# Merged mask and maximum products in a second attention, and one-hot tiles moved from VectorE to GpSimd

## What is computed

```python
a = _mha(inputs, inputs, inputs, Wk1, Wv1, Wq1, Wo1, bo1, masked=True)    # 256 x 256, causal, 16 heads
a = _layernorm(inputs + a, g1, b1)
c = _mha(context_seq, context_seq, a, Wk2, Wv2, Wq2, Wo2, bo2, masked=False)
c = _layernorm(c + c, g2, b2)
...
probs = softmax(x @ w_router)                  # 8 experts, top 1 of them used, the 8th adds nothing
out = 2 * top_value * expert(x)[top_index]     # 7 routed experts, hidden 512
return out + (x @ ws_up * silu(x @ ws_gate)) @ ws_down
```

## Time and profile before

| what | us |
|---|---|
| median of 3 runs | 335.74 (334.33 to 340.63) |
| the profiled execution | 338.23 |
| its span, first to last instruction | 336.1 |
| TensorE busy | 291.7 (87%) |
| VectorE busy | 257.9 (77%) |
| ScalarE busy | 209.6 (62%) |
| GpSimd busy | 152.2 (45%) |
| mean granted TensorE clock | 0.946 of full speed |

### The profile page before, as it was taken

The page is one execution under the profiler, slowest core; times in us unless marked ns, Lnnn a source line. Parts: engine busy times, 40 slices in busy tenths (PEclk is TensorE's granted clock), DMA queues, the critical chain, the costliest instruction groups (busy, mean ns, idle before and its releaser), DMA issues.

```text
span 336.1 us, 8921 instructions
## 1 busy us (share of the span) xinstructions
PE 291.7 (87%) x3475; PEld 222.8 (66%) x3475; DVE 257.9 (77%) x694; ACT 209.6 (62%) x442; POOL 152.2 (45%) x157
## 2 busy tenths in 40 slices
PE   5787957599999998989998999775898999999994
PEld 5655746455656645777776787544655999759993
DVE  4699977874664897977999577789689996894832
ACT  3665973445469649777867999234763648745561
POOL 9902898546344111443434345312431666432551
PEclk9999976958999999997999999799699999999998
DMA  7600223522400000000000000000002202040211
GB/s 249 252 2 1 97 96 100 180 98 91 137 0 2 0 0 4 2 2 2 2 2 3 2 2 3 2 0 0 3 3 108 82 4 97 2 168 21 90 41 32
DMA packets 6609, 16.64 MB, mean 50 GB/s; under 512 B 676, under 2 KB 2984, under 8 KB 6568
## 3 DMA queue, kind: packets, MB, share of 16 engines
q1 hardware_dynamic: 6568, 16.08, 13.6%
HBM read 10.83 MB, written 0.52 MB: 34 GB/s over the span
## 4 chain that ended last, share of the span: by engine, by line
PE 52%; DVE 31%; ACT 5%; POOL 4%; issue 4%; DMA 1%; SPq 0%; DVEq 0%; ACTq 0%
PE ps L808 8%; PE ps L810 7%; PE ps L809 7%; DVE MX L1400 6%; PE ps L1037 5%; DVE prl L667 3%; DVE stat L1355 2%; POOL prl L667 2%; PE ps L869 2%; PE ps L1129 2%; PE ps L870 2%; PE ps L881 2%; PE ps L1025 2%; PE ps L1099 2%; DVE pr L1576 2%
## 5 line engine op out<-in xcount | busy, mean ns | idle before, releaser
L667 POOL TENSOR_TENSOR prl<-pr,prh 128x384 f16<-128x384 f32 (+1 forms) x48 | 49.4, 1029 | 76.0 <-ACT pr L1188 76.0
L1185 ACT ACTIVATE prh<-ps 128x384 f16<-128x384 f32 (+1 forms) x96 | 51.2, 534 | 17.6 <-PE ps L810 6.6
L1400 DVE TENSOR_REDUCE MX<-ps 128x8 f32<-128x512 f32 (+2 forms) x80 | 52.1, 682 | 8.3 <-PE ps L911 4.5
L672 POOL TENSOR_TENSOR prl<-pr,prh 128x512 f16<-128x512 f32 x28 | 32.7, 1171 | 43.6 <-ACT prh L1225 43.6
L777 POOL TENSOR_TENSOR wl<-wraw,wh 128x512 f16<-128x512 f32 (+1 forms) x30 | 33.5, 1137 | 18.1 <-DVE wh L1288 18.0
L667 DVE TENSOR_TENSOR prl<-ps,prh 128x384 f16<-128x384 f32 (+1 forms) x48 | 28.5, 594 | 6.3 <-ACT ps L1188 5.9
L1576 DVE TENSOR_TENSOR pr<-ps,hr 128x512 f32<-128x512 f32 x28 | 19.0, 685 | 11.9 <-ACT hr L1219 10.7
L819 PE MATMUL ps<-cst 128*128 128x128 f32 x120 | 21.9, 321 | 4.7 <-DMA cst<-in_const 4.1
L1188 ACT ACTIVATE ps<-ps 128x384 f32<-128x384 f32 (+1 forms) x48 | 25.8, 538 | 0.0
L1188 ACT ACTIVATE pr<-ps 128x384 f32<-128x384 f32 (+1 forms) x48 | 25.6, 533 | 0.0
L1219 ACT ACTIVATE hr<-ps 128x512 f32<-128x512 f32 x28 | 16.5, 597 | 13.6 <-PE ps L810 12.8
(11 more groups left out here) (256 smaller groups left out, 1045.2 us busy)
## 6 DMA issues: line engine op xcount, KB each, us to landing
wraw<-in_weights SPq DMA_DIRECT2D x8, 768.0 KB, 4.0
wraw<-wh SPq DMA_DIRECT2D x6, 384.0 KB, 2.6
wraw<-wl SPq DMA_DIRECT2D x6, 384.0 KB, 3.0
wraw<-in_weights SPq DMA_DIRECT2D x2, 576.0 KB, 7.3
rowb<-in_rows SPq DMA_DIRECT2D x1, 708.0 KB, 4.6
wd<-in_down SPq DMA_DIRECT2D x1, 576.0 KB, 7.3
X<-in_x SPq DMA_DIRECT2D x2, 256.0 KB, 4.0
picks<-in_spread SPq DMA_DIRECT2D x1, 512.0 KB, 5.0
```

The source lines that it names most:

```text
L667: return engine.tensor_tensor(prl[:, g, three, 0:width], whole, prh[:, g, three, 0:width], ALU.subtract)
L672: return engine.tensor_tensor(hlo[:, g, k % NPV, :], hh[:, g, k % 2, :], hhi[:, g, k % NPV, :], ALU.subtract)
L1185: nc.scalar.activation(high, src[:, 0:width], ACT.Exp, scale=SCALE[a]).then_inc(pr_ready, 1)
L1400: nc.vector.tensor_reduce(o, src[:].rearrange("p (h k) -> p h k", h=heads), AX_X, ALU.max).then_inc(max_read, 1)
```

## The change

1. In the second attention the two mask products (columns 0 and 256) become one matmul of 2 x 128 columns, and the two that add the negated maxima become one of 384 columns. For that MT holds 384 columns, with the last 128 queries twice; `negmax` makes the third block with one more matmul, and its copy on ScalarE is 384 wide where a = 1. The columns in all stay the same.
2. `onehot_t` is issued by GpSimd, as the same tensor_scalar with the same waits. In the cost table it stands as 1.0 on GpSimd instead of 0.42 on VectorE.

```diff
--- before.py
+++ after.py
@@ -256,7 +256,7 @@
             "split_low": [("pool", 1.25)], "plow_pool": [("pool", .95 if e[1:2] == (1,) else 1.22)], 
             "lo1": [("pool", 1.17)], "xsplit": [("act", .6), ("pool", 1.2)], "rank": [("pe", .5), ("dve", 2.6)],
             "onehot": [("dve", 2.2)], "spill": [("dve", 1.2)], "sort_high": [("pe", .87), ("act", .6)], "sort_low": [("pe", .87), ("dve", .7)],
-            "spots": [("pe", .25), ("act", .6)], "onehot_t": [("dve", .42)],
+            "spots": [("pe", .25), ("act", .6)], "onehot_t": [("pool", 1.0)],
             "downr": [("pe", .72), ("act", .29), ("dve", .3)], "back": [("pe", .52)],
             "turn": [("pe", .95), ("act", 1.2 if e[1:2] in (("x1",), ("x3",)) else .6), ("dve", .69)], "v1": [("pe", .8), ("act", .65), ("dve", .69)], "bias_split": [("dve", 1.6)], "square": [("pe", 1.), ("dve", .69 if e[1:2] != ("v1",) else 1.45)],
             "negmax": [("dve", .6), ("pe", .3), ("act", .4)], "pv": [("pe", .3)], "out_norm": [("dve", .78)],
@@ -531,7 +531,7 @@
         VS = [sb("VSh", [P, G, T, H, DV], F16), sb("VSl", [P, G, T, H, DV], F16)]
         MX = sb("MX", [P, B, 2, H])
         MP = sb("MP", [P, B, 2, P], BF16)
-        MT = sb("MT", [P, B, S], BF16)
+        MT = sb("MT", [P, B, S + P], BF16)
         pr = sb("pr", [P, G, 2, GT])
         prh = sb("prh", [P, G, NPV, GT], F16)
         prl = sb("prl", [P, G, NPV, GT], F16)
@@ -783,6 +783,13 @@
                     g = e[1]
                     pool.wait_ge(x_high, n)
                     nc.gpsimd.tensor_tensor(xhl[g][:, 1], lnx[:, g], xhl[g][:, 0], ALU.subtract).then_inc(x_ready, 1)
+                elif kind == "onehot_t":
+                    _, g, s = e
+                    pool.wait_ge(spots_ready, nth[("spots", g)])
+                    for kind_, done in (("sort_high", sorted_high_mm), ("sort_low", sorted_low_mm)):
+                        pool.wait_ge(done, 3 * (g + 1))
+                    nc.gpsimd.tensor_scalar(onehot_t[:, s, :], spotsT[g], consts("part", 10)[:, s:s + 1], None,
+                                            ALU.is_equal).then_inc(onehot_t_ready, 1)
                 elif kind == "plow_pool":
                     pool.wait_ge(prh_ready, nth[("scores",) + e[1:]])
                     make_low(nc.gpsimd, e).then_inc(prl_ready[kind], 1)
@@ -932,8 +939,8 @@
                     pe.wait_ge(masks1_ready, 1)
                     pe.wait_ge(neg_ready, n)
                     take(bank[e][0], negT_ready, n)
-                    for t in range(2):
-                        mm = nc.tensor.matmul(o[:, t * P:(t + 1) * P], MP[:, e[2], t, :], identb[:], start=True, stop=True)
+                    for i, t in enumerate((0, 1, 1) if e[1] == 1 else (0, 1)):
+                        mm = nc.tensor.matmul(o[:, i * P:(i + 1) * P], MP[:, e[2], t, :], identb[:], start=True, stop=True)
                     mm.then_inc(neg_mm, 1)
                 elif kind == "scores":
                     _, a, b, u = e
@@ -952,7 +959,7 @@
                                              KBX[:, p // 2, b, 2 * (p % 2):2 * (p % 2) + 2, :].rearrange("p h k -> p (h k)"),
                                              QS[:, g, p // 2, q0:q0 + S], start=True, stop=False)
                             mm = nc.tensor.matmul(o[:, i * S:(i + 1) * S],
-                                                  pairsel[:, 2 * p:2 * p + 2, :].rearrange("p h k -> p (h k)"), mt,
+                                                  pairsel[:, 2 * p:2 * p + 2, :].rearrange("p h k -> p (h k)"), mt[:, 0:S],
                                                   start=False, stop=True)
                     else:
                         kb = kbs[:, b % 2]
@@ -960,10 +967,9 @@
                         kw = dict(start=False, stop=True, skip_group_check=True)
                         nc.tensor.matmul(o[:, 0:S], kb[:, j, h, 0:P], QS[:, g, j, q0:q0 + S], start=True, stop=True)
                         nc.tensor.matmul(o[:, S:S + P], kb[:, j, h, P:2 * P], QS[:, g, j, q0 + P:q0 + S], **kw)
-                        nc.tensor.matmul(o[:, 0:S], headsel[:, u:u + 1].broadcast_to([P, P]), mt, **kw)
-                        nc.tensor.matmul(o[:, S:S + P], headsel[:, u:u + 1].broadcast_to([P, P]), mt[:, P:S], **kw)
-                        for c in (0, S):
-                            mm = nc.tensor.matmul(o[:, c:c + P], identb[:], trib[:, 1, :], **kw)
+                        nc.tensor.matmul(o[:, 0:S + P], headsel[:, u:u + 1].broadcast_to([P, P]), mt, **kw)
+                        mm = nc.tensor.matmul(o[:].rearrange("p (c k) -> p c k", k=S)[:, :, 0:P], identb[:],
+                                              trib[:, 1, :].unsqueeze(1).broadcast_to([P, 2, P]), **kw)
                     mm.then_inc(sc_mm, 1)
                 elif kind == "pv":
                     _, a, b, u = e
@@ -1172,7 +1178,8 @@
                     nc.scalar.copy(VS[0][:, g, :, :, 0:D], src[:].rearrange("p (t h d) -> p t h d", t=T, d=D)).then_inc(v1_high, 1)
                 elif kind == "negmax":
                     sc.wait_ge(neg_mm, n)
-                    nc.scalar.copy(MT[:, e[2], :], src[:, 0:S]).then_inc(negT_ready, 1)
+                    width = S + P if e[1] == 1 else S
+                    nc.scalar.copy(MT[:, e[2], 0:width], src[:, 0:width]).then_inc(negT_ready, 1)
                 elif kind == "scores":
                     _, a, b, u = e
                     g = b // 2
@@ -1527,13 +1534,6 @@
                     for t in range(T):
                         ins = nc.vector.tensor_scalar(onehot[:, t, :], slots, pos[:, t:t + 1], None, ALU.is_equal)
                     ins.then_inc(onehot_ready, 1)
-                elif kind == "onehot_t":
-                    _, g, s = e
-                    dve.wait_ge(spots_ready, nth[("spots", g)])
-                    for kind_, done in (("sort_high", sorted_high_mm), ("sort_low", sorted_low_mm)):
-                        dve.wait_ge(done, 3 * (g + 1))
-                    nc.vector.tensor_scalar(onehot_t[:, s, :], spotsT[g], consts("part", 10)[:, s:s + 1], None,
-                                            ALU.is_equal).then_inc(onehot_t_ready, 1)
                 elif kind == "sort_low":
                     j = e[2]
                     width = min(GT, SLOTS - j * GT)
```

## The result

| what | before | after |
|---|---|---|
| median (4 runs each) | 335.3 (334.33 to 340.63) | 354.62 (351.46 to 355.52) |
| ratio after/before, 95% | | 1.055 (1.049 to 1.062) |
| the profiled execution | 338.23 | 355.52 |
| its span | 336.1 | 353.3 |

The account below looks back on a forecast made before the run. The prediction took TensorE, with VectorE behind it, to bound the kernel. Its terms 0.1 + 1.0 + 1.2 + 1.55 + 0.4 gave 4.25, say +4.2 us on the median 335.74: 339.9 us, range 334 to 346.5.

Parts of the forecast that it names:

- Part 2: Twenty one-hot tiles move from VectorE to GpSimd at 1.0 us each (ends 0.24 and 1.2); VectorE loses 10.2 us.
- rival of GpSimd as the bound: Late routed stretches: one-hot tiles cost more than GpSimd's room, decisive from 1.6 us each; 346.1 us at 2.0; chance 0.17.
- (a): Group 0's routed tiles: one-hot tiles delay low halves on GpSimd, less 0.5 us for VectorE's relief; 1.0 us slower.
- the 0.4 of group 1: Group 1's routed tiles: one-hot tiles ahead of low halves on GpSimd delay down products; about 0.4 us slower.
- (b): Start of group 1's sorts: less TensorE work covers the wait for the onehot operations; 1.2 us more idle.
- (c): End of group 1: a downr and two back steps go ahead of the last up1, lengthening the tail by 1.55 us.
- Part 1: Second attention: merged matmuls keep 1024 columns a unit; 0.1 us slower, bounds -0.6 and +0.65.
- rival that a removed matmul gives back its spacing: Second attention: 128 removed matmuls give back 0.055 us each, 7.0 us, for 332.9 us; chance 0.04.
- Relief: At 0.7 us a tile or less, GpSimd's delays vanish and 3.0 us of TensorE idle return: 335.6 us; chance 0.25.
- VectorE isn't relieved: Group 1's gate1, rank and onehot: VectorE waits for begun GpSimd operations, three meetings of 1 us: 342.9 us; chance 0.09.

Follow-up runs that it names:

- new order with 288 columns: The changed kernel, each GpSimd one-hot tile made over its first 288 columns only (1.01 us): 345.6 us, one run; routed stretches 77.49 us against 71.12 before.
- new order on VectorE: The changed kernel's step order, but VectorE makes the one-hot tiles at their planned times: 342.5 us, ratio 1.016 to the kernel before.
- old order: Step order of the kernel before, products merged, one-hot tiles on GpSimd: 354.9 us, ratio 1.056; at 0.45 us a tile (64 columns only) 333.4, one run.
- merging alone: The kernel before with only the merged matmuls, one-hot tiles on VectorE at their old cost: 334.7 us, ratio 0.997.
- one-hot alone: The kernel before with only the one-hot tiles moved to GpSimd and their cost entry changed, no merged matmuls: 352.3 us, ratio 1.042.

## Why the prediction was wrong

**The step that failed is the price in Part 2**, "one operand less, so it stands nearer to the 1.17 row: I take 1.0 us". Measured: 1.566 in the kernel. The reasoning was by operands, from another operation; the rows were tensor_tensor (1.17 us at 512 columns) and a tensor_scalar of 4 columns, and these hold no slope for tensor_scalar. Calling the tensor_tensor a bound from above was the mistake, since no row tied the price to the number of operands. This one number brings 8.5 of the 14.9 us (77.49 to 85.99 at the same order). At my own price the loss in A and B is 6.4 us for the 4.15 of my sum, and 335.3 + 6.4 = 341.7 us lies inside my range. (The one whole time at that price, 345.6 beside 332.9, is 12.6 apart; what goes beyond the 6.4 lies ahead of A, which starts as late as 261.26 there.)

**What hung on it.** The rival of GpSimd as the bound had the right mechanism, but "decides from 1.6 us each" was wrong too: at 1.566 it already costs 8.5 us. I had divided the free time of a stretch by ten. In B the queue can't start before the sixth sort (315.98, 4.67 us after the first), and up1 steps stand behind down products and back steps that wait, so the room is smaller than the difference of sums, as the equal 4.5 us of pauses show. It was given 0.17, and the range ended at 346.5, just above that rival's own 346.1.

**(a) and the 0.4 of group 1, delays at 1.0 us: 1.4 forecast, none measured.** The new order with 288 columns stands at 77.49 against 77.47 with the tiles on VectorE. The delay is there and the net isn't: with 288 columns the first down product behind the two tiles starts at 265.86, 4.60 us into A, where it was 3.79 before (264.17 - 260.38), 0.8 us late for my 0.7. But with the tiles on VectorE TensorE waits 0.76 us for VectorE a little further on, and this wait is gone with them on GpSimd: relief gives back here what GpSimd delays (at 0.45 us relief shows alone, 1.5 us). My estimate of single low halves was right in kind, as the first one of group 0 shows after: two tiles from 263.95, the low half at 267.04, 4.30 us behind the first up1 of the tile (262.74) where it was 2.17 (262.55 - 260.38). It was the net that I had as a loss.

**(b) and (c), the order: 2.75 forecast, 6.35 measured.** The gap ahead of the sorts is there, but smaller than forecast:

```profile
311.31 4.50 PE L1105 MATMUL ps<-route,lni 128*128 128x512 f16 x24 [0.90 <-DVE route L1535]
```

TensorE waits 0.90 us for the one-hot where it waited 0.17 before, 0.7 us more for my 1.2. The tail is there as well: the last up1 ends at 343.75 and the last downr starts at 347.20, 3.45 us for the 3.46 forecast. In the new order on VectorE B grew by 0.71 us though two down1 steps (1.34) had moved from it into A, so by 2.05 of its own, for my 1.55. A grew by 5.64: 1.34 of those down1 steps, 0.7 of (b), and some 3.6 that no term of mine has. 0.7, 2.05 and 3.6 are the 6.35. Of the 3.6, 2.1 are idle time of TensorE; the rest isn't traced further. The new order on VectorE shows in A, busy by stretch:

```profile
259.77:304.73 44.96, 40.45 (x600) 34.94 (x598) 36.61 (x115) 26.69 (x54) 23.85 (x22) 1.00 0.18 70
```

and in its waits over the same stretch:

```profile
ACT prh L1232 <- DVE pr L1583: 10.0, 10, 2.2
...
PE ps L1105 <- DVE route L1535: 0.9, 1, 0.9
PE ps L815 <- DVE act L1555: 0.8, 2, 0.5
PE ps L815 <- DVE tL L1331: 0.8, 1, 0.8
PE ps L815 <- POOL prl L679: 0.7, 2, 0.4
PE ps L1112 <- DVE pos L1521: 0.6, 1, 0.6
PE ps L815 <- DVE pr L1583: 0.5, 1, 0.5
PE ps L1135 <- DVE act L1555: 0.2, 1, 0.2
```

TensorE idles 4.5 us instead of 1.6, in nine gaps of 0.15 to 0.9 us, and ScalarE waits 10.0 us for the products of VectorE instead of 4.2. VectorE ended 3.8 of the 4.5 us. I had looked at two places of the order and taken the rest as equal. Which of the moved steps makes these gaps was not tried by a run of its own and stays open.

**Part 1 was right**: 0.1 us forecast, 0.997 measured with an interval of 0.992 to 1.003, and late stretches equal to 0.03 us. The rival that a removed matmul gives back its spacing is excluded: 7.0 us would have been 0.979. The Trainium skill's gap of 81 ns for a 128-column matmul ("TensorE: Matmul & The Clock Gate", Back-to-back issue gap) doesn't hold in this stream, whose rows have 0.05 us.

**Relief (0.25) is excluded too**, and by more than the price: even at 0.45 us a tile the old order gains 0.05 us in its 71, and the new order gets back 1.5 us of its 6.4 where I had put 3.0. **"VectorE isn't relieved" is half true**: its busy time fell by 7.1 us instead of 10.2, and where the other 3 us went isn't shown. But in the four onehot operations of group 1, one of the places where this rival wanted a further meeting with GpSimd, there is none: they take 719 ns each after and 717 before.

No version beat the kernel before by more than its measurement is uncertain. The best of the changed ones is merging alone, which takes the time of the kernel before.

## What to carry to other kernels

Before work moves to another engine, the price of exactly that operation form is to be measured there, by a few instructions of it at the end of a kernel that already runs; a neighbour's price, even of one with more operands, is no bound. An in-order queue doesn't fill up evenly: in the new order here the net cost of the engine was zero at 1.01 us a tile and rose by three quarters of each further microsecond, long before GpSimd's busy share looked high (51%). And where a planner reads a table, a changed entry moves everything else: the reshuffle alone cost 6.4 us, and another entry gave an order with 10 of the 14.9 us back, with no instruction faster. So the order is to be measured by itself, with the operation left where it was.

## What was not expected of the hardware

- On GpSimd a tensor_scalar of 128x512 takes 1.56 us, a tensor_tensor 1.15, a copy 0.61; 16 or 32 bits and comparison or subtraction change it by less than 1%; a number as its operand instead of a column takes 1.49.
- Four matmuls of 1024 columns in all take what six do, 0.43 against 0.44 us: in this stream the instruction has no price beside its columns.
- With long idle gaps of TensorE (single waits of 5 us) the mean granted clock of the routed stretches was 0.88 to 0.90. A gap of 2.2 us left it at 1.00 in the execution of after, and was followed by 3.4 us at the lower level in that of the one-hot alone, with the same order: 48.57 us against 49.84.
